# Row-sum reciprocals and router weights as float16 halves in an attention and expert kernel on one core

## The reference

```python
x = x + attention(layernorm(x), ...)      # 16 heads, relative_k and relative_v added
h = layernorm(x)
shared = sum over the 2 shared experts of gelu(h @ sw1 + sb1) @ sw2 + sb2, halved
gates = h @ router_w + router_b            # 8 columns
topv, topi = top_k(gates, 2); probs = softmax(topv)
moe = sum over the chosen 2 of probs * (gelu(h @ w1 + b1) @ w2 + b2)
x = x + shared + moe
```

## Time and profile before

| what | value |
|---|---|
| median of 3 runs | 2102.9 us (2101.99 to 2104.03) |
| the profiled execution | 2102.11 us, its span 2100.3 us |
| granted TensorE clock, mean | 0.993 |
| PE busy | 98% of the span |
| DVE, ACT, POOL busy | 76%, 72%, 57% |
| attention stage | to about 1618 us |
| expert stage | about 482 us, one batch some 30.4 us |

### The profile page before, as it was taken

One profiled execution on the slowest core, in us unless ns is written; L12 is line 12 of the kernel. 1 busy time (PEld: TensorE's weight loads), 2 busy tenths in 40 slices (PEclk: granted clock), 3 DMA queues, 4 the chain that ended last, 5 costly groups with the idle time before them and its releaser, 6 DMA issues.

```text
span 2100.3 us, 88112 instructions
## 1 busy us (share of the span) xinstructions
PE 2053.3 (98%) x37378; PEld 1531.0 (73%) x37378; DVE 1598.9 (76%) x3746; ACT 1514.3 (72%) x3304; POOL 1206.7 (57%) x1271
## 2 busy tenths in 40 slices
PE   3999999999999999999999999999999999999999
PEld 1677777777777777777777777777777777777777
DVE  4787787789778877877897788778876666666665
ACT  3666676766776667667667666666666988898887
POOL 5464555445445645464455456345443888888887
PEclk7999999999999999999999999999999999999999
DMA  5112211221131122212221321222121221122120
GB/s 142 34 46 67 79 52 52 71 76 56 55 87 46 56 68 75 56 46 68 75 56 45 88 66 52 60 77 55 47 63 37 27 30 27 23 25 30 22 28 12
DMA packets 255680, 114.47 MB, mean 55 GB/s; under 512 B 142218, under 2 KB 251156, under 8 KB 255348
## 3 DMA queue, kind: packets, MB, share of 16 engines
q1 hardware_dynamic: 255348, 109.60, 21.3%
HBM read 83.34 MB, written 8.39 MB: 44 GB/s over the span
## 4 chain that ended last, share of the span: by engine, by line
PE 96%; DVE 1%; POOL 1%; SPq 1%; ACT 1%; issue 0%; DMA 0%; ACTq 0%; DVEq 0%; POOLq 0%
PE ps L1425 21%; PE ps L1360 12%; PE ps L1445 10%; PE ps L1455 9%; PE ps L1367 9%; PE ps L1378 7%; PE ps L1634 3%; PE ps L1636 3%; PE ps L1635 3%; PE ps L1616 3%; PE ps L1618 3%; PE ps L1617 3%; PE ps L1463 1%; PE ps L1341 1%; PE ps L1316 1%; PE ps L1336 1%
## 5 line engine op out<-in xcount | busy, mean ns | idle before, releaser
L688 ACT ACTIVATE probs<-ps,neg_max 128x512 f32<-128x512 f32 x1024 | 690.5, 686 | 354.7 <-DVE neg_max L892 354.6
L892 DVE TENSOR_REDUCE neg_max<-ps 128x1 f32<-128x512 f32 x1024 | 635.9, 683 | 148.9 <-PE ps L1367 144.6
L499 POOL TENSOR_TENSOR stat_hi<-q_twice,mask8h 128x1024 f16<-128x1024 f16 x128 | 242.7, 1896 | 657.2 <-PE ps L1367 594.3
L1425 PE MATMUL ps<-const,probs 128*128 128x128 f32 x4096 | 496.0, 274 | 1.7 <-ACT probs L688 1.4
L1425 PEld LDWEIGHTS ps<-const,probs 128*128 128x128 f32 x4096 | 452.6, 141 | 30.2 <-issue 15.3
L897 DVE COPY probs_t<-ps 128x512 f32<-128x512 f32 x512 | 339.6, 683 | 89.3 <-PE ps L1425 86.7
L678 ACT ACTIVATE probs_t<-ps 128x512 f32<-128x512 f32 x512 | 278.8, 595 | 132.7 <-PE ps L1425 130.5
L609 POOL TENSOR_TENSOR probs_t<-probs,probs_t 128x1024 f16<-128x1024 f32 x160 | 338.2, 2136 | 31.8 <-ACT probs_t L771 31.5
L1360 PE MATMUL ps<-keys,stat_hi 128*32 128x512 f16 x4096 | 318.1, 383 | 0.0
L1163 DVE SCALAR_TENSOR_TENSOR keys<-ps,comb,keys 128x128 f32<-128x128 f32 x640 | 179.6, 343 | 137.1 <-PE ps L1636 137.1
L1367 PE MATMUL ps<-rk_split,stat_rel 96*32 96x512 f16 (+2 forms) x4096 | 281.5, 340 | 0.0
(11 more groups left out here) (157 smaller groups left out, 2878.6 us busy)
## 6 DMA issues: line engine op xcount, KB each, us to landing
rv_step<-in_rv_win SPq DMA_DIRECT2D x128, 512.0 KB, 3.8
keys<-keys SPq DMA_DIRECT2D x64, 96.0 KB, 2.7
x_pair<-in_x SPq DMA_DIRECT2D x8, 512.0 KB, 4.4
q_twice<-q_hi SPq DMA_DIRECT2D x32, 128.0 KB, 2.9
q_lo_pair<-q_lo SPq DMA_DIRECT2D x32, 128.0 KB, 2.6
rel_scratch<-rel_t SPq DMA_DIRECT2D x256, 16.0 KB, 3.2
x_pair<-in_x SPq DMA_DIRECT2D x16, 256.0 KB, 3.1
x_pair<-rel_scratch SPq DMA_DIRECT2D x64, 64.0 KB, 4.0
```

The costliest lines, as they stand in the source:

```text
L688: nc.scalar.activation(probs[:, q, :], ps[:, i, :], ACT.Exp, bias=neg_max[:, q:q + 1], accum_out=row_sum[parity][:, s * QUADS + q:s * QUAD ...
L892: nc.vector.tensor_reduce(neg_max[:, q:q + 1], ps[:, i, :], op=ALU.max, axis=AX_X, negate=True).then_inc(max_done, 1)
L1425: last = nc.tensor.transpose(ps[:, bank, rt * P:(rt + 1) * P], probs[:, q, rt * P:(rt + 1) * P], ident)
```

## The change

Three things change.

1. **Reciprocals.** They are made in place in `row_sum`, scaled by 1024 and stored as two float16 halves (`inv_all` has two planes): one instruction of VectorE becomes three, with two waits. The 0/1 tables are float16 and scaled by 1/1024. The spread is now 8 float16 products, written in rows of 128 columns (query row of the quad outermost). The division reads that bank in order and reads and writes the attention sums in every fourth column (`by_query`).
2. **Router.** Its weights are scaled by 64 and split into float16 halves side by side (16 columns). Each 128 rows of h take two float16 products (high half of h, low half of h) in place of one float32 product. VectorE adds the two halves and the bias with two instructions and a wait between.
3. **Place.** `prepare_gates` on TensorE moves from behind the down products of e = 5 to behind the up products that follow (in e = 6, ahead of that expert's down), and waits for the low half of h.

Setup gets one more small instruction on VectorE (`head_scaled`), and two more ahead of the last pair (`rw_split`).

```diff
+INV_SCALE = 1024.0
...
         rw_s = sb("rw_s", [P, NE])
+        rw_split = sb("rw_split", [P, 2, NE], F16)
         rb_row = sb("rb_row", [P, NE])
...
         row_sum = [sb(f"row_sum{i}", [P, STEPS * QUADS]) for i in range(2)]
-        inv_all = sb("inv_all", [P, PAIRS * STEPS * QUADS])
-        head_rows = sb("head_rows", [P, 2, H])
...
+        inv_all = sb("inv_all", [P, 2, PAIRS * STEPS * QUADS], F16)
+        head_rows, head_scaled = sb("head_rows", [P, 2, H]), sb("head_scaled", [P, 2, H])
         probs = sb("probs", [P, QUADS, L])
...
-        spread_rows = [a[:].bitcast(F32).rearrange("p (l h d) -> p l h d", l=QT, h=H) for a in (q_hi, q_lo)]
+        spread_rows = [a[:, 0:QT * D].rearrange("p (l h d) -> p l h d", l=QT, h=H) for a in (q_hi, q_lo)]
         rel_nat = x_pair[:, TPB:2 * TPB, :].rearrange("p t (h d) -> p t h d", h=H)
...
-        SETUP_DVE = 9
+        SETUP_DVE = 10
...
+            def by_query(cols):
+                return cols.rearrange("p (c l) -> p l c", l=QT)
...
             def first_sums(bank):
...
                 dve.wait_ge(inv_t_done, START + 1)
-                nc.vector.tensor_tensor(o_sum_t, ps[:, bank, :], o_sum_t, ALU.mult).then_inc(o_ready, 1)
+                nc.vector.tensor_tensor(by_query(o_sum_t), ps[:, bank, :].rearrange("p (l c) -> p l c", l=QT), by_query(o_sum_t), ALU.mult).then_inc(o_ready, 1)
             def first_residual(bank):
...
             def first_gates(bank):
                 dve.wait_ge(gate_done, START + 1)
-                nc.vector.tensor_tensor(gates[:], ps[:, bank, 0:TPB * NE].rearrange("p (t e) -> p t e", t=TPB),
-                                        rb_row[:].unsqueeze(1).broadcast_to([P, TPB, NE]), ALU.add).then_inc(ffn_link, 1)
...
-            first_links = Links(ffn_link, 5)
+                sums = ps[:, bank, 0:TPB * 2 * NE].rearrange("p (t a e) -> p t a e", t=TPB, a=2)
+                nc.vector.scalar_tensor_tensor(gates[:], sums[:, :, 0, :], 1.0 / W_SCALE, rb_row[:].unsqueeze(1).broadcast_to([P, TPB, NE]),
+                                               ALU.mult, ALU.add).then_inc(ffn_link, 1)
+                dve.wait_ge(ffn_link, START + 5)
+                nc.vector.scalar_tensor_tensor(gates[:], sums[:, :, 1, :], 1.0 / W_SCALE, gates[:], ALU.mult, ALU.add).then_inc(ffn_link, 1)
...
+            first_links = Links(ffn_link, 6)
             def spread_heads():
...
                 for b in range(2):
-                    nc.vector.tensor_tensor(spread_rows[b], head_rows[:, b, :].unsqueeze(1).unsqueeze(3).broadcast_to([P, QT, H, DK]),
+                    nc.vector.tensor_tensor(spread_rows[b], head_scaled[:, b, :].unsqueeze(1).unsqueeze(3).broadcast_to([P, QT, H, DK]),
                                             m4.unsqueeze(2).unsqueeze(3).broadcast_to([P, QT, H, DK]), ALU.mult).then_inc(spread_ready, 1)
             def reciprocals(pair, parity):
                 dve.wait_ge(exp_done, START + (pair + 1) * TILES)
-                nc.vector.reciprocal(inv_all[:, bass.ds(pair * STEPS * QUADS, STEPS * QUADS)], row_sum[parity][:]).then_inc(inv_done, 1)
...
+                nc.vector.reciprocal(row_sum[parity][:], row_sum[parity][:]).then_inc(inv_link, 1)
+                high, low = (inv_all[:, a, bass.ds(pair * STEPS * QUADS, STEPS * QUADS)] for a in range(2))
+                dve.wait_ge(inv_link, START + pair * 2 + 1)
+                nc.vector.tensor_scalar(high, row_sum[parity][:], INV_SCALE, None, ALU.mult).then_inc(inv_link, 1)
+                dve.wait_ge(inv_link, START + pair * 2 + 2)
+                nc.vector.scalar_tensor_tensor(low, row_sum[parity][:], INV_SCALE, high, ALU.mult, ALU.subtract).then_inc(inv_done, 1)
             def last_step(pair, parity):
...
-            FFN_LINKS = 8
+            FFN_LINKS = 9
             def prepare_attention(b, link):
...
                 dve.wait_ge(inv_t_done, START + b + 1)
-                nc.vector.tensor_tensor(o_sum_t, ps[:, 1, :], o_sum_t, ALU.mult).then_inc(o_ready, 1)
+                nc.vector.tensor_tensor(by_query(o_sum_t), ps[:, 1, :].rearrange("p (l c) -> p l c", l=QT), by_query(o_sum_t), ALU.mult).then_inc(o_ready, 1)
             def prepare_residual(b, slot, link):
...
             def prepare_gates(b, link):
                 dve.wait_ge(gate_done, START + b + 1)
-                link(nc.vector.tensor_tensor(gates[:], ps[:, 1, 0:TPB * NE].rearrange("p (t e) -> p t e", t=TPB),
-                                             rb_row[:].unsqueeze(1).broadcast_to([P, TPB, NE]), ALU.add))
+                sums = ps[:, 1, 0:TPB * 2 * NE].rearrange("p (t a e) -> p t a e", t=TPB, a=2)
+                link(nc.vector.scalar_tensor_tensor(gates[:], sums[:, :, 0, :], 1.0 / W_SCALE, rb_row[:].unsqueeze(1).broadcast_to([P, TPB, NE]),
+                                                    ALU.mult, ALU.add))
+                link.wait()
+                link(nc.vector.scalar_tensor_tensor(gates[:], sums[:, :, 1, :], 1.0 / W_SCALE, gates[:], ALU.mult, ALU.add))
                 choice_tops(link)
...
                 nc.vector.tensor_tensor(bk_far_col[:], bks_col[:], rk_last_col[:], ALU.add).then_inc(setup_dve, 1)
+                nc.vector.tensor_scalar(head_scaled[:], head_rows[:], 1.0 / INV_SCALE, None, ALU.mult).then_inc(setup_dve, 1)
                 nc.vector.tensor_tensor(rk_split[32:64, :], rk3[32:64, :], rk_split[32:64, :], ALU.subtract).then_inc(setup_dve, 1)
...
                 nc.vector.tensor_scalar(b2_split[32 * row:32 * row + EXPERTS, :], b2_s[:], W_SCALE, None, ALU.mult).then_inc(w_low, 1)
-            dve.wait_ge(w_low, 4)
+            nc.vector.tensor_scalar(rw_split[:, 0, :], rw_s[:], W_SCALE, None, ALU.mult).then_inc(w_low, 1)
+            dve.wait_ge(w_low, 5)
             nc.vector.scalar_tensor_tensor(b2_split[64:64 + EXPERTS, :], b2_s[:], W_SCALE, b2_split[0:EXPERTS, :], ALU.mult, ALU.subtract).then_inc(w_low, 1)
+            nc.vector.scalar_tensor_tensor(rw_split[:, 1, :], rw_s[:], W_SCALE, rw_split[:, 0, :], ALU.mult, ALU.subtract).then_inc(w_low, 1)
             pair_steps(PAIRS - 1, 1, False, False)
...
                 elif piece == "gates":
-                    pe.wait_ge(ffn_link, START + 5)
+                    pe.wait_ge(ffn_link, START + 6)
             def next_scores_wait(pair, s, j, first, ahead):
...
-                pe.wait_ge(w_low, 5)
+                pe.wait_ge(w_low, 7)
                 up(0, 0, 0)
...
             def spread_reciprocals(b, parity, pair, bank):
...
                 for l in range(QT):
-                    last = nc.tensor.matmul(ps[:, bank, :].rearrange("p (c l) -> p l c", l=QT)[:, l, :],
-                                            spread_rows[parity][:, l, :, :].rearrange("p h d -> p (h d)"),
-                                            inv_all[:, bass.ds(pair * STEPS * QUADS, STEPS * QUADS)], start=True, stop=True, skip_group_check=True)
+                    for low in range(2):
+                        last = nc.tensor.matmul(ps[:, bank, l * P:(l + 1) * P], spread_rows[parity][:, l, :, :].rearrange("p h d -> p (h d)"),
+                                                inv_all[:, low, bass.ds(pair * STEPS * QUADS, STEPS * QUADS)], start=low == 0, stop=low == 1)
                 last.then_inc(inv_t_done, 1)
             def prepare_attention(b, parity, pair):
...
                     pe.wait_ge(bias_added, START + b)
-                pe.wait_ge(h_ready, START + 2 * b + 1)
...
+                pe.wait_ge(h_low, START + b + 1)
                 for t in range(TPB):
-                    last = nc.tensor.matmul(ps[:, bank, t * NE:(t + 1) * NE], h_t[:, slot, t * P:(t + 1) * P], rw_s[:], start=True, stop=True)
+                    cols = slice(t * P, (t + 1) * P)
+                    out = ps[:, bank, t * 2 * NE:(t + 1) * 2 * NE]
+                    halves_of = rw_split[:].rearrange("p a e -> p (a e)")
+                    nc.tensor.matmul(out, h_hi[:, slot, cols], halves_of, start=True, stop=False)
+                    last = nc.tensor.matmul(out, h_lo[:, slot, cols], halves_of, start=False, stop=True)
                 last.then_inc(gate_done, 1)
             def prepare_comb(b, slot):
...
                         up(b + 1, 1 - slot, e + LOOK - EXPERTS)
+                    if ahead and e == 6:
...
+                        prepare_gates(b + 1, 1 - slot, 1)
                     down(b, slot, e)
...
                             prepare_h(b + 1, 0)
-                        if e == 5:
-                            prepare_gates(b + 1, 1 - slot, 1)
                     if e == 1:
```

More of the change, by code:

```diff
@@ L231, in attention_ffn @@
         nat_tr, q_split_low, v_ready = sem("nat_tr"), sem("q_split_low"), sem("v_ready")
-        dve_link, ln_link = sem("dve_link"), sem("ln_link")
+        dve_link, ln_link, inv_link = sem("dve_link"), sem("ln_link"), sem("inv_link")
         k_low_ready, q_low_ready, v_far_ready = sem("k_low_ready"), sem("q_low_ready"), sem("v_far_ready")
@@ L263, in attention_ffn @@
         KEY_COPIES = 12
```

(2 more changed lines are left out.)

## The result

| | before | after |
|---|---|---|
| median of the runs, us | 2102.62 (2101.99 to 2104.03, 4 runs) | 2090.84 (2089.8 to 2091.74, 4 runs) |
| ratio to before | 1 | 0.9943, 95% interval 0.9926 to 0.996 |
| profiled execution: time, span, us | 2102.1, 2100.3 | 2090.2, 2088.1 |

The forecast was 2091.5. The rest of this document takes them apart.

What follows compares the result with a forecast made beforehand. TensorE was taken to bound the kernel (busy 98% of the span). Terms -16.8 + 1.5 + 3.4 + 0.35 + 0.1 = -11.4 us took the profiled 2102.1 to 2090.7; with 0.8 for the median, 2091.5 us, range 2085.5 to 2097.5.

Steps and rivals of the forecast that it cites:

- The spread: TensorE's spread of the reciprocals as eight float16 products takes 0.45 us in place of 0.89, saving 0.44 us a batch.
- The router: TensorE's router products take 0.25 us in place of 0.86, saving 0.61 us a batch, with 0.41 to 0.76 as ends.
- rival 2: Router products held by issue at 56 ns each: 2094.7 us, chance 0.11; at 107 ns, no saving: 2101.3, chance 0.01.
- The division at Wo: TensorE's Wo product waits about 0.1 us for VectorE's division of 1.05 to 1.41 us: 1.5 us lost in 15 batches.
- rival 1: VectorE's division takes 1.41 us and TensorE waits 0.23 us at Wo in 15 batches: 2093.5 us, chance 0.17.
- The pair starts: In attention, two more VectorE instructions ahead of the maxima make TensorE wait 0.48 us at seven starts: 3.4 us lost.
- the slack of 0.30: At a pair start in attention, 0.30 us of VectorE's 0.78 us delay would not reach TensorE.
- the 0.15 us for GpSimd: Added to VectorE's delay at a pair start, because GpSimd has an instruction on SBUF when the scaling would start.
- Rival 3: Pair starts cost nothing, as ScalarE's exponentials catch up or the instructions are shorter: 2088.1 us, chance 0.13.
- The moved router products and the second gates instruction at nothing: In the expert stage, TensorE's later router products and VectorE's extra gates instruction (0.23 us) are covered and cost no time.
- rival 4: ScalarE or GpSimd takes over as TensorE speeds up, through a wait not found: about 2101 us, chance 0.06.
- The prediction's own signs: Batch period of 29.9 us or more, VectorE division over 1.5, or expert 9's down products waiting for GpSimd would disprove it.

Runs made afterwards that it cites:

- e3: The changed kernel, but with the float16 spread written in every fourth column and VectorE dividing in order: 2101.7 us.
- e8: As e3, but with the output bias added to x a batch ahead: 2093.9 us, batch period 29.71 us.
- e11: The changed kernel with both split instructions of the reciprocals done twice at each pair start: 2095.8 us, pairs 195.27 us.
- e10: The changed kernel with the router products back behind the down products of expert 5: 2100.6 us.
- e1: Kernel before with the router part alone (halves and new place); spread, reciprocals and division as before: 2099.7 us.
- e4: The changed kernel with the output bias added to x a batch ahead, out of the path from Wo to the statistics: 2087.8 us.
- e5: Kernel before with only the output bias added to x a batch ahead: 2102.5 us, batch period 30.39 us.

## Why the prediction came out right, and where it was not

By the forecast's own steps:

- **The spread:** 0.45 us, as forecast. The sentence that rows of the bank or every fourth column make no difference that a row shows held for the rows there were, but the chip makes one of 0.42 us (e3, e8), as much as the step's whole gain. The Trainium skill states it, page "SBUF — State Buffer", section "Door 1: The DMA port swizzle (why `[64,N]` ≈ `[32,N]`)", in its note on cachelines: access to PSUM that is not contiguous slows matmuls significantly. The 109 ns a product against 56 in float16 agree; the float32 products, 111 ns each in columns, show no such cost against those with Wo.
- **The router:** 0.20 us rather than 0.25, start to start 25 to 26 ns. The lower part of the range was right, and rival 2 fell with both its prices. The 25 ns that the prediction cites from the Trainium skill, page "TensorE: Matmul & The Clock Gate", section "Wait — 56ns, not 53.3ns?", agree; the 107 ns a load of its section "LDWEIGHTS (loading the stationary operand)" do not. 16 x 0.05 = 0.8 us better.
- **The division at Wo:** it takes 1.12 us, in the range of 1.05 to 1.41. No wait at Wo appears, so the 1.5 us were not lost, and rival 1 fell. Groups of VectorE of the changed kernel, expert stage:

```profile
L1132 DVE TENSOR_TENSOR xn_t<-ps,xn_t 128x512 f32<-128x512 f32 x13 | 14.6, 1124 | 0.4
```

- **The pair starts:** 3.4 us forecast for seven, 1.5 lost in the six pairs that can be measured from start to start (0.25 us each; the rows of the first give 0.17). Timeline of the changed kernel at the place of the earlier trace rows:

```profile
255.70 0.93 DVE L1092 RECIPROCAL row_sum<-row_sum 128x128 f32<-128x128 f32 x1
...
256.67 0.26 DVE L1095 TENSOR_SCALAR inv_all<-row_sum 128x128 f16<-128x128 f32 x1
256.96 0.29 DVE L1097 SCALAR_TENSOR_TENSOR inv_all<-row_sum,inv_all 128x128 f16<-128x128 f32 x1
257.17 2.48 DVE L896 TENSOR_REDUCE neg_max<-ps 128x1 f32<-128x512 f32 x4
...
259.45 1.16 PE L1363 MATMUL ps<-w_qkv_s,xn_t 128*128 128x128 f32 x8
```

  The maxima start 1.47 us after the reciprocal, where it was 0.97: 0.50 later, not 0.78. TensorE's L1363 starts 3.75 after it, where it was 3.58. So the slack of 0.30 was right (0.50 - 0.17 = 0.33), and e11 confirms that it is used up; the term was mis-sized by the 0.15 us for GpSimd, of which at most 0.05 came (the scaling takes 0.26 us, 0.21 forecast), and by the subtraction: the maxima start 0.21 us after it, while it still runs. Rival 3 was half right.
- **The moved router products and the second gates instruction at nothing:** right by the rows: no wait for the low half of h, and but one of the down products for GpSimd in the whole stage. Without the move the change is worth about 2 us (e10).
- **What failed is a step that the prediction took as granted in its first paragraph:** that a microsecond taken from TensorE is a microsecond of time "as long as no other engine gets late". Only rival 4 questioned it, with ScalarE's mean load (26.8 of 29.4 us a batch) as the argument. Mean load could not show it: GpSimd's wait of 1.95 us for the statistics made a loop of 30.26 us, hidden 0.13 us under TensorE's 30.39. The row was there before, 13 waits of equal length for the same releaser, beside a bias addition of 1.37 us for 0.76 us of work. It cost 4.5 us, half of what rival 4 feared. A reading that fits the rows is that the full gain of 1.10 us brought the addition ahead of the fourth subtraction every second time: a short batch leaves GpSimd without its idle 1.95 us, its next fourth subtraction comes early again, and the addition loses.
- **The prediction's own signs:** it named a batch period of 29.9 or more as one that would prove it wrong. Seven of 14 periods are 29.93; their mean, 29.61, lies above its 29.4 to 29.5. By this sign its account of the batches was wrong although its time was right. The other two did not appear: no division over 1.5 us, and of the down products only that one wait, of 0.6 us, for GpSimd.

Sum against before, in the traces: the stretch from batch 1 to batch 15 is 425.5 us before and 414.6 after, -10.9, where the forecast's terms give -14.7 and 1.4 back at Wo, -13.3. The opening up to the second pair is 0.8 us shorter, which no changed instruction explains; six pairs +1.5; the last pair, which holds batch 0's router products, -0.7; from the last reciprocal to batch 1 -0.4; the end from batch 15 on -0.8 (together -12.2, the difference of the spans, but for rounding). Missed: +4.5 for the loop. Feared in vain: 1.5 at Wo, 1.9 at pair starts, 0.8 at the router. That these cancel to 0.7 us is luck. Counted by the forecast's own terms the router part alone gives 16 x 0.61 - 0.35 = 9.4 us, and e1 brought 3.

## What to carry to other kernels

Before a saving on the leading engine is counted in full, look for waits on the other engines that repeat with one fixed length every iteration. They can be links of a loop, and its length is a floor that mean loads don't show. Not each is one: GpSimd's wait of 0.37 us for the choice stands in every batch of e4 too, where TensorE's full gain comes all the same. Here shortening TensorE by 0.44 or 0.65 us a batch gave 0.04% (within noise) and 0.14%, by both 0.57%, and with the loop opened by one moved addition 0.7%, while that addition moved on its own gave nothing (e5). An experiment that undoes one part of a change measures that part only if the floor isn't reached; otherwise move the floor first.

## What the hardware showed that was not expected

- Float16 products of 128 columns that write every fourth column of a PSUM bank go at about 0.87 / 8 us = 109 ns each, in rows at 56 ns. Full-width float16 weights with 16 streamed columns go at 25 ns, product to product.
- VectorE's division with a strided read of SBUF and a strided write (every fourth word) takes 1124 ns for 512 elements, in order 691.
- One VectorE addition with both inputs in SBUF took 0.76, 1.37 or 2.50 us in these kernels, by where its start lay against GpSimd's subtraction: 0.15 us ahead, 1.3 us behind, 0.15 us behind. When it came second it ended 0.54 us after that subtraction. In the changed kernel this order of two starts decided 0.64 us of a batch.
